# Attention and a dequantizing feed-forward on one core: the unpacking work of the weights at other places of the pairs

## What is computed

```
x = x + attn(layernorm(x))       # 16 heads, chunks of 128 tokens, decay, rotary q and k, gated norm
x = x + ffn(layernorm(x))
# ffn: Wg, Wu (4096 x 512), Wd (512 x 4096), 4-bit codes, one scale for 32 values
gate, up = x @ Wg.T, x @ Wu.T
gelu = tanh(0.79788 * (gate + 0.044715 * gate**3)) * gate * 0.5 + gate * 0.5
out  = (gelu * up) @ Wd.T
```

## Time and profile before

| | |
|---|---|
| median of 3 runs | 1391.69 us (1389.89 to 1393.22) |
| the profiled execution, its own time | 1391.66 us |
| its span, first to last instruction | 1389.5 us |
| mean granted TensorE clock | 0.98 |
| busy share: PE, weight loads, VectorE, ScalarE, GpSimd | 94%, 77%, 84%, 39%, 45% |
| first feed-forward product (L1335) | about 341 us from the start |

### The profile page before, as it was taken

How to read it: one execution, slowest core, us unless ns; L and a number is a source line. 1 busy time by engine, 2 the same in 40 slices (tenths; PEclk the granted TensorE clock), 3 DMA queues, 4 the chain that set the end, 5 groups by cost and what they waited for, 6 DMA issues and landing times.

```text
span 1389.5 us, 20001 instructions
## 1 busy us (share of the span) xinstructions
PE 1311.0 (94%) x6796; PEld 1065.6 (77%) x6796; DVE 1172.0 (84%) x1778; ACT 542.8 (39%) x925; POOL 621.2 (45%) x488
## 2 busy tenths in 40 slices
PE   8899999997799999999999999999999999999998
PEld 5688877885687877878787878778787878787877
DVE  7798998898697979797988979797979788897975
ACT  5233343333444334343333444334333433344431
POOL 2433564466344535263544445452625354354531
PEclk9899999998999999999999999999999999999999
DMA  9000000000010000000000001000000000000003
GB/s 308 4 1 8 17 9 1 1 1 1 5 40 17 31 21 31 15 30 23 23 23 29 23 23 30 15 30 23 30 17 28 23 23 23 30 25 20 31 6 116
DMA packets 21774, 40.17 MB, mean 29 GB/s; under 512 B 2660, under 2 KB 2916, under 8 KB 21604
## 3 DMA queue, kind: packets, MB, share of 16 engines
q1 hardware_dynamic: 21060, 39.47, 8.5%
q10 hardware_dynamic: 672, 0.13, 0.0%
HBM read 35.40 MB, written 4.19 MB: 28 GB/s over the span
## 4 chain that ended last, share of the span: by engine, by line
PE 38%; issue 30%; DVE 15%; POOL 14%; ACT 3%; POOLq 0%; DVEq 0%; ACTq 0%
PE bank L1193 6%; POOL hl L1158 5%; PE bank L1335 5%; PE bank L1194 5%; PE bank L1195 5%; PE bank L1338 5%; PE bank L1337 5%; POOL wgl L1075 3%; POOL wdl L1082 3%; DVE stg L725 2%; PE bank L1207 2%; DVE stg L717 1%; PE bank L1283 1%; DVE bank L914 1%; PE bank L1300 1%
## 5 line engine op out<-in xcount | busy, mean ns | idle before, releaser
L1158 POOL TENSOR_TENSOR hl<-hx,hh 128x512 fp32r<-128x512 f32 x128 | 180.1, 1413 | 362.3 <-ACT hh L508 362.3
L1335 PE MATMUL bank<-xoh,wgh 128*128 128x512 f32 x448 | 180.6, 403 | 38.6 <-DVE cxa L914 30.5
L906 DVE TENSOR_TENSOR acc<-acc,bank 128x512 f32<-128x512 f32 x248 | 167.5, 680 | 51.4 <-PE bank L1195 50.5
L1193 PE MATMUL bank<-wdh,hh 128*128 128x512 f32 x512 | 203.9, 398 | 4.1 <-DVE acc L906 4.1
L1194 PE MATMUL bank<-wdl,hh 128*128 128x512 f32 x512 | 202.6, 396 | 0.0
L1195 PE MATMUL bank<-wdh,hl 128*128 128x512 f32 x512 | 201.7, 394 | 0.0
L1338 PE MATMUL bank<-xoh,wgl 128*128 128x512 f32 x448 | 178.2, 398 | 0.0
L1337 PE MATMUL bank<-xol,wgh 128*128 128x512 f32 x448 | 177.7, 397 | 0.0
L1335 PE MATMUL bank<-xoh,wuh 128*128 128x512 f32 x448 | 175.7, 392 | 1.6 <-ACT cxa L497 1.6
L1337 PE MATMUL bank<-xol,wuh 128*128 128x512 f32 x448 | 174.5, 389 | 0.0
L1338 PE MATMUL bank<-xoh,wul 128*128 128x512 f32 x448 | 174.4, 389 | 0.0
(11 more groups left out here) (161 smaller groups left out, 2715.8 us busy)
## 6 DMA issues: line engine op xcount, KB each, us to landing
stg<-packed_dram SPq DMA_DIRECT2D x48, 256.0 KB, 2.6
stg<-scales_dram SPq DMA_DIRECT2D x48, 256.0 KB
out_dram<-acc SPq DMA_DIRECT2D x16, 256.0 KB, 2.0
acc<-x_dram SPq DMA_DIRECT2D x3, 1024.0 KB, 13.9
w_in<-wq_dram SPq DMA_DIRECT2D x2, 512.0 KB, 5.9
w_in<-wk_dram SPq DMA_DIRECT2D x2, 512.0 KB, 7.6
w_in<-wv_dram SPq DMA_DIRECT2D x2, 512.0 KB, 9.1
w_in<-wo_dram SPq DMA_DIRECT2D x2, 512.0 KB, 11.9
```

Source lines behind the costliest of these rows:

```text
L906: V.tensor_tensor(row, row, BY[j % 2][:], ALU.add).then_inc(y_add, 1)
L1158: nc.gpsimd.tensor_tensor(hl[n][:], hx[n][:], hh[n][:].bitcast(F32), ALU.subtract).then_inc(h_lo[n], 1)
L1193: pe.matmul(dst, w_h, x_h, start=start, stop=False)
L1335: pe.matmul(dst[:], w_h, x_h, start=start and a == 0, stop=False, skip_group_check=True)
```

## The change

No instruction is added or taken away (two waits and the loop's bookkeeping apart), and PE's and SP's streams stay as they are. What moves:

- VectorE, pair p = 0: product C21 goes behind the total of GB; bits DOWN ahead of gelu(C11); scale DOWN behind y(3); bits of the next round's GATE behind y(5); scale UP leaves this pair.
- VectorE, pair p = 1: scale GATE ahead of y(0); bits UP behind y(3), ahead of gelu(C22); scale UP behind prod(C11).
- VectorE, both: prod(C12), arg(C21), gelu(C22), gelu(C21), arg(C12) and gelu(C12) lie later among the y.
- ScalarE: `high_of`(C22) ahead of the first copy; `wide_hi` of UP one instruction earlier per half; tanh of C21 ahead of C22; `wide_hi` of GATE ahead of the copy of UA into cxa; tanh(C12) behind that copy; `high_of`(C12) later.
- GpSimd: in p = 0 no sums, `wide_lo` of UP ahead of `low_of`(C12); in p = 1 sums of GATE ahead of `low_of`(C12), `wide_lo` of GATE ahead of `low_of`(C11), sums of UP at the end.
- Bits of unit k now wait for the scaling of unit k-1 (dq_f).
- The first tiles: on ScalarE `tanh_qk(1)` and `gate_low(1)` come ahead of `norm1(2)` and `wo_hi`; on VectorE the bn_stats of tiles 4 to 15 are taken four to an attention tile in t = 1, 2, 3, and `stats_r` of tiles 8 to 15 one tile later.

```diff
@@ VectorE, unit_bits_a
             dve.wait_ge(s_pk, 16 * k + 16)
+            wait(dve, dq_f, k)
@@ VectorE, first tiles
-            dve.wait_ge(s_x[1], 16)
-            stats(4, 2 * CHUNKS)
             silu_qk(1)
...
-                if t in (1, 2, 3):
-                    if t < 3:
-                        dve.wait_ge(s_x[t + 1], 16)
-                    first = {1: 8, 2: 10, 3: 14}[t]
-                    stats(first, first + 2)
+                if 1 <= t < CHUNKS:
+                    dve.wait_ge(s_x[t], 16)
+                    stats(4 * t, 4 * t + 4 - 2 * (t == 2))
@@ ScalarE, pair
+                if not first:
+                    wait(act, y_ps, 8 * P_ - 8)
+                    high_of(C22, P_ - 1)
...
                 copy(cxb[:], GA, g_copy)
+                if p == 0 and not ready:
+                    act.wait_ge(u_ps, 14 * q)
+                    wide_hi(3 * q + UP, 2 * q + UP, wuh, 0)
                 tanh_of(C11, P_)
...
                 square_of(C12, GC, P_)
+                if p == 1 and not last:
+                    act.wait_ge(g_ps, 7 * P_ + 7)
+                    for piece in range(2):
+                        wide_hi(3 * q + 3 + GATE, 2 * q + 2 + GATE, wgh, piece)
                 x1(18, 19)
-                tanh_of(C12, P_)
                 act.wait_ge(u_ps, 7 * P_ + 1)
                 act.wait_ge(h_gelu[C22], P_ + 1)
                 copy(cxa[:], UA, u_copy)
                 x1(20, 21)
+                tanh_of(C12, P_)
@@ VectorE, pair
                 total(GB[:], GB, hx[C11][:], g_sum)
+                if not done:
+                    up_21(P_ - 1)
                 if not first:
                     up_12(P_ - 1)
                 arg(C11, GB, P_)
...
+                if p == 0 and not ready:
+                    unit_bits(3 * q + DOWN)
...
+                gelu(C11, GB, P_)
+                dve.wait_ge(g_copy, 3 * P_ + 3)
+                total(cxa[:], GC, hx[C22][:], g_sum)
+                if p == 1 and not last:
+                    unit_scale(3 * q + 3 + GATE)
+                y(0)
...
+                y(3)
+                if p == 0 and not ready:
+                    unit_scale(3 * q + DOWN)
                 if p == 1 and not last:
-                    unit_scale(3 * q + 3 + GATE)
+                    unit_bits(3 * q + 3 + UP)
                 x1(18, 19)
+                gelu(C22, cxa, P_)
+                y(4)
+                gelu(C21, GA, P_)
...
+                y(5)
+                if p == 0 and not ready and not last:
+                    unit_bits(3 * q + 3 + GATE)
...
                 prod(C11, UB, P_)
-                y(5)
                 if p == 1 and not last:
-                    unit_bits(3 * q + 3 + UP)
+                    unit_scale(3 * q + 3 + UP)
                 y(6)
@@ GpSimd, pair
                     low_of(C21, P_ - 1)
-                    if p == 0 and not ready:
-                        unit_sums(3 * q + UP, 2 * q + UP)
-                    low_of(C12, P_ - 1)
+                    if p == 1 and not last:
+                        unit_sums(3 * q + 3 + GATE, 2 * q + 2 + GATE)
                     if p == 0 and not ready:
                         wide_lo(3 * q + UP, wuh, wul)
+                    low_of(C12, P_ - 1)
                 if p == 1 and not last:
-                    unit_sums(3 * q + 3 + GATE, 2 * q + 2 + GATE)
+                    wide_lo(3 * q + 3 + GATE, wgh, wgl)
                 low_of(C11, P_)
                 if p == 1 and not last:
-                    wide_lo(3 * q + 3 + GATE, wgh, wgl)
+                    unit_sums(3 * q + 3 + UP, 2 * q + 2 + UP)
```

More of the change, by code:

```diff
@@ L424, in _ @@
             tanh_gate(0)
+            tanh_qk(1)
+            gate_low(1)
             norm1(2, 2)
             wo_hi()
-            tanh_qk(1)
-            gate_low(1)
             def x1t_hi_(g):
@@ L519, in x1 @@
                             x1t_hi_(g)
+                if not first:
+                    wait(act, y_ps, 8 * P_ - 8)
+                    high_of(C22, P_ - 1)
+                if p == 1 and not ready:
+                    act.wait_ge(y_ps, 16 * q)
+                    down_hi(3 * q + DOWN, 0)
                 act.wait_ge(g_ps, 7 * P_ + 1)
@@ L523, in pair @@
                 copy(hx[C11][:], GA, g_copy)
+                if p == 1 and not ready:
+                    down_hi(3 * q + DOWN, 1)
                 if not first:
[L525 to L529, removed]
                     high_of(C21, P_ - 1)
-                    if p == 1 and not ready:
-                        down_hi(3 * q + DOWN, 1)
                 act.wait_ge(g_sum, 3 * P_ + 1)
@@ L553, in pair @@
                 square_of(C21, GA, P_)
-                if p == 0 and not ready:
-                    wide_hi(3 * q + UP, 2 * q + UP, wuh, 1)
-                tanh_of(C22, P_)
+                if not first:
+                    high_of(C12, P_ - 1)
                 x1(16, 17)
                 tanh_of(C21, P_)
+                tanh_of(C22, P_)
                 act.wait_ge(g_sum, 3 * P_ + 3)
@@ L567, in pair @@
                 x1(20, 21)
+                tanh_of(C12, P_)
+                act.wait_ge(u_ps, 7 * P_ + 3)
+                copy(cxb[:], UA, u_copy)
                 wait(act, y_ps, 8 * P_ - 4)
                 high_of(C11, P_)
[L570 to L577, removed]
+                x1(22, 23, 24, 25)
                 act.wait_ge(u_ps, 7 * P_ + 5)
@@ L937, in up_22_21, with up_21 @@
                 prod(C22, cxa, pair)
+            def up_21(pair):
                 dve.wait_ge(u_ps, 7 * pair + 6)
@@ L958, in y @@
                         add_y(P_ - 1, 1 - p, j)
-                if not (ready and P_ <= 1):
-                    up_22_21(P_ - 1)
-                if p == 0 and not ready:
-                    unit_scale(3 * q + UP)
+                done = ready and P_ <= 1
+                if not done:
+                    up_22(P_ - 1)
                 dve.wait_ge(g_ps, 7 * P_ + 2)
@@ L974, in pair @@
                     prod(C12, UC, P_ - 1)
-                gelu(C11, GB, P_)
-                if p == 0 and not ready:
-                    unit_bits(3 * q + DOWN)
-                if p == 1 and not last:
-                    unit_bits(3 * q + 3 + GATE)
-                dve.wait_ge(g_copy, 3 * P_ + 3)
-                total(cxa[:], GC, hx[C22][:], g_sum)
-                y(0)
+                y(1)
                 arg(C22, cxa, P_)
-                y(1)
-                arg(C21, GA, P_)
-                gelu(C22, cxa, P_)
                 if first:
@@ L989, in pair @@
                     stats2(2)
-                x1(16, 17)
-                gelu(C21, GA, P_)
                 dve.wait_ge(g_ps, 7 * P_ + 7)
```

30 lines of the change are left out of this document (14 added, 16 removed).

## The result

The changed kernel takes **1409.99 us** (median; 1405.3 to 1411.82), the kernel before on the same chip 1391.99 us (1389.89 to 1393.22): ratio 1.0126, 95% interval 1.0097 to 1.0155. It is slower, as forecast (1419 us, range 1370 to 1430). The profiled execution took 1408.70 us, its span is 1406.6 us, its mean granted clock 0.985.

The account below looks back on a forecast made before the run. PE, busy 94% of the span, was taken to bound the kernel, so only its waits and lower clock could be won. Fifteen rounds (+28.5 us) and the start (-1) gave +27.5 on 1391.66: 1419 us, range 1370 to 1430.

Parts of the forecast that it names:

- slower, as forecast: Whole kernel: +1.9 us a feed-forward round, mainly a new PE wait at p = 1, step 17 (+3.25 us); slower given 0.58.

Follow-up runs that it names:

- experiment 5: Changed kernel with ScalarE's square of C12 in p = 1 cut into 128 and 384 columns: 1420.6 us, ratio 1.0204.
- experiment 7: Changed kernel with ScalarE's square of C12 in p = 1 cut into four pieces of 128 columns: 1375.22 us, ratio 0.9877.
- experiment 10: Changed kernel with the first tiles as in the kernel before: 1405.97 us, ratio 1.0112.
- experiment 6: Changed kernel with ScalarE's square of C12 (p = 1) and copy of GA into hx[C22] (p = 0) each cut into 128 and 384 columns: 1422.32 us.

## What to carry to other kernels

When a VectorE instruction with both operands in SBUF (or a fast one like the 0.42 us bit instructions) and a GpSimd subtraction are issued close together, work out which comes first, to some hundredths of a microsecond, from the instructions ahead on their own engines: the loser is held until the winner is done (2.55 to 2.66 us for 0.69 here), and what is queued behind it on its engine waits too. If the loser is on the path of TensorE, do not shave hundredths; put an instruction that has an operand in PSUM or waits for TensorE anyway on the other side of it (y(3) here), or move the conversion that releases GpSimd behind what TensorE wants, so that the two do not meet. And value a stop of TensorE by what it loses itself; keep the clock that may fall behind it as a separate, wide term.

## What the runs showed that I had not expected

- A ScalarE instruction cut in two delays what follows by 0.05 us only, though 128 columns take 0.26 us by themselves: the next is issued 0.16 us later (experiment 5). Four pieces give a delay of 0.15 us (experiment 7: the square's first piece starts at 841.96, the next instruction at 842.59, where 0.48 us lie between them uncut), and that turned the lead.
- Three kernels with nearly the same stops took 1405.97, 1409.99 and 1420.6 us (experiment 10, the changed kernel, experiment 5). The rounds and the part of the start that ran at the lower clock differ between them and are most of it where it was taken apart (experiment 5). In an experiment that leaves a 3 us stop in place, a difference of this size is not yet the edit's.
- Two edits that each remove one stop were not additive: 55.6 and 8.5 us apart, 81.2 together.
- GpSimd is held just as VectorE is when it comes second: its half of a wide weight took 2.54 to 2.56 us behind the last bit instruction in experiment 7 and 2.69 in the last round of experiment 6, for 2.12.
